# Attention with PV in batches of two key tiles

## Chip, cores, metric

One core of a Trainium2 chip runs the whole program. The time is the device time of one execution in microseconds (us), here the median of several executions.

## What is computed

One transformer layer with conditioning, for 8 sequences of 512 tokens, 512 channels wide, in float32. There are 16 query heads of 32 channels that share 4 key/value heads (four query heads to one key head, called a group below).

```
cond = silu(c) @ wc.T + bc
sh1, sc1, g1, sh2, sc2, g2 = split(cond)
h = ln(x) * (1 + sc1) + sh1
q, k, v = h @ wq.T, h @ wk.T, h @ wv.T
a = softmax(q k / sqrt(32));  attn = a v
x = x + g1 * (attn @ wo.T)
h = ln(x) * (1 + sc2) + sh2
x = x + g2 * (gelu(h @ w1.T + b1) @ w2.T + b2)
```

## The kernel before

A prologue makes the conditioning and turns the weights, then `attention` does all 8 sequences, then `mlp` does all 8. Only `attention` changes.

A sequence is 64 beats: 4 groups (one per key head), in each 4 key tiles `kt` of 128 keys, in each the 4 query heads `r`. Every engine has a `beat` function, and all run the same 64 beats in their own order, tied by semaphores. A beat of TensorE (PE) makes one bank of transposed scores (`scores`, 128 keys by 512 queries), which ScalarE (ACT) turns into `probs[kt]` with an exponential (`exp`), and one matmul of untransposed scores for a later group (`rows`), whose maximum VectorE (DVE) takes (`row_max`). Both sorts of score banks are double-buffered: the scores of beat n need the exponential of beat n-2, the row matmul of beat n the maximum of two rows before. The exponent subtracts the maxima inside the matmul: at beat 10 (`TURN_BEAT`) of a group TensorE turns the maxima of the next group (`turn_max`), ScalarE and VectorE split them into two parts (`max_high`, `max_low`), and at beat 11 ScalarE issues two DMAs (`stack_max`) that put them under `q_stack`, which the first scores of the next group need. A beat with nothing else is two matmuls.

`values` multiplies one key tile's `probs` with `v`: four heads, 32 columns each, into `pv_bank`, two matmuls a head. `sums` does the same with a matrix of ones and `probs_sum`, which GpSimd (POOL) adds up over the key tiles. Before, `values` of tile kt-1 runs in beat 1 of key tile kt (`PV_BEAT`), the last one in beat 1 of the next group, and `sums` behind the `values` of beat 5 (`SUM_AT` is (kt, r) = (1, 1)). `copy_pv` takes the finished bank, then `log_sums`, `invert`, `refine`, `reciprocal`, `divide`, `attn_high` and `attn_low` turn it into `attn`.

The table `FILL` says what else TensorE does in each beat, keyed by (group, key tile), one text per r. T0 to T3 turn the next sequence's x (ScalarE then does `modulate` and `h_high`, VectorE `h_low`), VT turns v, K, Q0 to Q3 and V are projections of the next sequence (Q3 of the present one), O0 to O3 the output projection of the sequence before; the letters a to d are quarters of a projection, three matmuls each. All use two `proj_bank` in the order in which they end, each waiting (`room`) until the one two before was taken. ScalarE takes them one beat after (`ACT_LAG`), VectorE two (`DVE_LAG`); h has lags of two and three. `STATS_AT`, `MOMENTS_AT`, `EPS_AT`, `SHIFT_AT` and `NORM_AT` are the beats (0 to 63) in which the normalization of the sequence after the next is done on VectorE, ScalarE and GpSimd.

The SyncE (SP) queue holds, in order: the copies of k and q into their stacks (`stack_k`, `stack_q`, 12 DMAs each for q), the load of the next x, in group 3 the store of x1 (`store_x1`), and when it has landed the load of the next `resid` (`load_resid`, 1 MB).

Of the kernel before, what the change touches and what calls it, by code (L numbers as in the profile page):

```python
# [16 lines left out]
HKV, R, HD = 4, 4, 32  # L17
DFF = 2048
TT = N // P
# [16 lines left out]


FILL = {
    (0, 0): ("VT", "", "", "Q3abcd"),
    (0, 1): ("T0", "", "", ""),  # L40
    (0, 2): ("T1", "", "T2", ""),
    (0, 3): ("", "", "T3", "O0ab"),
    (1, 0): ("", "O0c", "O0d Ka", ""),
    (1, 1): ("Kb", "", "Kcd", "O1abc"),
    (1, 2): ("O1d", "", "Q0ab", "Q0c"),
    (1, 3): ("", "", "", "Q0d O2a"),
    (2, 0): ("", "", "O2b", "O2c"),
    (2, 1): ("O2d", "", "O3a", "O3b"),
    (2, 2): ("", "O3c", "", "O3d Q1a"),
    (2, 3): ("", "", "Q1bc", "Q1d Q2a"),  # L50
    (3, 0): ("", "", "", "Q2bc"),
    (3, 1): ("", "", "Q2d", ""),
    (3, 2): ("Va", "Vb", "", "Vc"),
    (3, 3): ("", "Vd", "", ""),
}
GROUP = TT * R
PV_BEAT = 1
PV_COPY = 2
SUM_AT = (1, 1)
LN_AT = (2, 0)  # L60
INVERT_AT = (2, 0)
REFINE_AT = (2, 2)
RECIP_AT = (2, 2)
DIVIDE_AT = (2, 3)
# [3 lines left out]
TWO_ROWS = 6  # L68
ACT_LAG, DVE_LAG, COPY_LAG, TURN_LAG = 1, 2, 2, 3
STATS_AT = (40, 41, 43, 44)  # L70
MOMENTS_AT = 47
EPS_AT = 47
SHIFT_AT = 52
NORM_AT = (54, 55, 59, 63)
COND_AT = 2
RESID_AFTER = {0: (0,), 1: (1,), 2: (2, 3)}
# [65 lines left out]
def seq_units(b, has_last, has_next):  # L142
    ahead = before_units().after()
    if has_last:
        ahead = Units(seq_order(False, True), ahead).after()
        step = sizes(seq_order(True, True))
        ahead = {k: (b - 1) * step[k] + ahead[k] for k in ahead}
    return Units(seq_order(has_last, has_next), ahead)


def after_units():
    return Units(["O0", "O1", "O2", "O3"], seq_units(B - 1, True, False).after())
# [315 lines left out]
def attention(nc, f32, f32r, ALU, ACT, AX, sb, ps, sem, as_f32, seq_dram, ident, cond_cols, neg_half, norm_bufs, norm_sems,  # L468
# [3 lines left out]
    with ExitStack() as st:  # L472
# [23 lines left out]
        proj_taken = {"act": sem("proj_taken_act"), "dve": sem("proj_taken_dve")}  # L496
# [16 lines left out]
        def group_no(b, g):  # L513
            return b * HKV + g
# [8 lines left out]
        def exps_no(b, g, kt):  # L523

            return b * (HKV * TT * R) + (g * TT + kt) * R
# [4 lines left out]
        def rowed(b, g, has_next):  # L530

            if g < HKV:
                return b, g
            return (b + 1, g - HKV) if has_next else None
# [16 lines left out]
        with nc.Block() as block:  # L551
# [136 lines left out]
            def _(act):  # L688
# [121 lines left out]
                def beat(b, n, u, has_last, has_next, odd):  # L810

                    g, (kt, r) = n // GROUP, divmod(n % GROUP, R)
                    prev = (b, g - 1) if g > 0 else (b - 1, HKV - 1) if has_last else None
                    first_group = (g == 1 and not has_last)
                    after_turn = rowed(b, g + 1, has_next)
                    exp(b, g, kt, r, has_last)
                    if n % GROUP == TURN_BEAT and after_turn:
                        max_high(*after_turn)
                    if n % GROUP == TURN_BEAT + 1 and after_turn:
                        stack_max(*after_turn)  # L820
                    if prev and (kt, r) == (0, PV_COPY):
                        copy_pv(*prev, is_first=first_group)
                    if prev and (kt, r) == LN_AT:
                        log_sums(*prev, is_first=first_group)
                    if prev and (kt, r) == INVERT_AT:
                        invert(*prev)
                    if prev and (kt, r) == HIGH_AT:
                        if g == 2 and has_last:
                            act.wait_ge(proj_ready, u.ready("O3"))
                        attn_high(*prev, odd)  # L830
                    if n == COND_AT:
                        copy_cond(b + 1)
                    if n == EPS_AT and has_next:
                        add_eps(b + 2)
                    if n == SHIFT_AT and has_next:
                        shift_of(b + 2)
                    if n in NORM_AT and has_next:
                        norm(b + 2, NORM_AT.index(n))
                    for name in ended(n - COPY_LAG, has_last, has_next):
                        if name[0] == "T":  # L840
                            h_high(b + 1, u, int(name[1]))
                    for name in ended(n - ACT_LAG, has_last, has_next):
                        if name == "VT":
                            take_vt(b, u, has_last)
                        elif name == "V":
                            take_v(u)
                        elif name[0] == "T" and has_next:
                            modulate(b + 1, u, int(name[1]))
                        elif name[0] == "T":
                            modulate(b + 1, u, int(name[1]), scale=SC2, shift=SH2)  # L850
                        elif name == "K":
                            k_high(b + 1, u)
                        elif name[0] == "Q":
                            q_high(b if name == "Q3" else b + 1, int(name[1]), u)
# [15 lines left out]
            def _(dve):  # L870
# [101 lines left out]
                def beat(b, n, u, has_last, has_next, odd):  # L972
                    g, (kt, r) = n // GROUP, divmod(n % GROUP, R)
                    prev = (b, g - 1) if g > 0 else (b - 1, HKV - 1) if has_last else None
                    if n == MOMENTS_AT and has_next:
                        dve.wait_ge(stats_done, b * TT + 3 * TT)
                    for row in rows_in(b, n, has_next):
                        if row[2] < ROWS:
                            row_max(*row)
                    if n == MOMENTS_AT and has_next:  # L980
                        moments(b + 2)
# [42 lines left out]
            def _(pe):  # L1024
# [86 lines left out]
                def values(b, g, kt, is_first=False):  # L1111

                    pe.wait_ge(exp_done, exps_no(b, g, kt) + R)
                    if kt == 0 and not is_first:
                        pe.wait_ge(pv_copied, group_no(b, g))
                    for r in range(R):
                        last = nc.tensor.matmul(pv_bank[HD * r:HD * r + HD, :], v[:, kt, g * HD:g * HD + HD],  # L1117
                                                probs[kt][:, r, :], start=(kt == 0), stop=(kt == TT - 1))
                    last.then_inc(pv_done, 1)

                def sums(b, g, is_first=False):

                    pe.wait_ge(added, group_no(b, g) * (TT - 1) + (TT - 1))
                    if not is_first:
                        pe.wait_ge(attn_split, group_no(b, g))
                    for r in range(R):
                        last = nc.tensor.matmul(sum_bank[HD * r:HD * r + HD, :], ones[:, :], probs_sum[:, r, :],
                                                start=True, stop=True)
                    last.then_inc(sums_ready, 1)
# [33 lines left out]
                def beat(b, n, u, has_last, has_next, odd):  # L1163
                    g, (kt, r) = n // GROUP, divmod(n % GROUP, R)
                    prev = (b, g - 1) if g > 0 else (b - 1, HKV - 1) if has_last else None
                    scores(b, g, kt, r, has_last)
                    for row in rows_in(b, n, has_next):
                        if row[2] < ROWS:
                            rows(*row)
                    if r == PV_BEAT and kt > 0:  # L1170
                        if (g, kt) == (0, 1):
                            pe.wait_ge(proj_taken["act"], u.taken("VT"))
                        values(b, g, kt - 1, is_first=not has_last and g == 0)
                    elif r == PV_BEAT and prev:
                        values(*prev, TT - 1)
                    for name, tiles in fill(n, has_last, has_next):
                        do(name, tiles, b, u, odd)
                    if (kt, r) == SUM_AT and prev:
                        sums(*prev, is_first=not has_last and g == 1)
                    for row in rows_in(b, n, has_next):  # L1180
                        if row[2] == ROWS:
                            turn_max(*row[:2])
# [5 lines left out]

                def after(b):
                    u = after_units()  # L1190
                    values(b, HKV - 1, TT - 1)
                    for tt in range(2):
                        out_part(b, tt, u, range(HKV - 1), True)
                    sums(b, HKV - 1)
                    for tt in range(2):
                        out_part(b, tt, u, range(HKV - 1, HKV), True)
                    for tt in range(2, TT):
                        out_part(b, tt, u, range(HKV), True)
# [309 lines left out]
```

## Time and profile before

| | |
|---|---|
| median of 3 runs | 1560.06 us (1552.71 to 1562.45) |
| the profiled execution | 1565.58 us, its span 1563.8 us |
| TensorE, VectorE, ScalarE, GpSimd busy | 95%, 51%, 40%, 37% |
| mean granted TensorE clock | 0.975 of full |

Busy shares are averages over the whole span; matmuls overlap, so their starts tell more than their durations. Times in rows are us from the start of the span.

### The profile page before, as it was taken

Reading aid. Unit: us, or ns where it says so; the run is one execution under the profiler, and the core shown is the slowest. Engines: PE = TensorE matmul, PEld = TensorE weight load, DVE = VectorE, ACT = ScalarE, POOL = GpSimd, SP = SyncE. Lnnn points to the kernel's source line nnn. Section 1 sums busy time; section 2 is a strip of 40 time slices with the busy share of each in tenths; the row PEclk is TensorE's granted clock in tenths of the full one; section 3 lists DMA queues with packets and bytes.
Section 4 is the critical chain, followed back from the end, with each engine's and each line's share of the span. In section 5 each row is a group of like instructions: output and inputs, shape, how many; then the busy total and the mean of one; then the engine's idle time right before and its main releaser. Section 6 shows DMA issues by size and latency. Waiting matters only on the chain. (4 is left out here: it accounts for less than half of the span.)

```text
span 1563.8 us, 19142 instructions
## 1 busy us (share of the span) xinstructions
PE 1481.9 (95%) x7013; PEld 1045.6 (67%) x7013; DVE 800.6 (51%) x1356; ACT 625.1 (40%) x1116; POOL 576.0 (37%) x222
## 2 busy tenths in 40 slices
PE   7889999998999999998979999999999999999996
PEld 4545556555656555654448888888788888878885
DVE  5377667776776677676544342332524242242421
ACT  5346656665575666666532322112111121211210
POOL 0027567675776677576710020110202021020202
PEclk9869999999999999999999999999999999999998
DMA  7132314233151313323053311010202001020100
GB/s 259 55 75 59 97 52 117 65 85 101 33 154 36 112 54 98 93 71 87 2 158 112 101 55 34 27 60 0 87 0 69 18 27 60 0 87 0 61 1 27
DMA packets 68309, 105.16 MB, mean 67 GB/s; under 512 B 10464, under 2 KB 19696, under 8 KB 68232
## 3 DMA queue, kind: packets, MB, share of 16 engines
q1 hardware_dynamic: 66192, 103.74, 21.7%
q8 instruction: 40, 0.66, 0.2%
q10 hardware_dynamic: 2048, 0.53, 0.2%
q14 instruction: 29, 0.24, 0.0%
HBM read 55.44 MB, written 16.81 MB: 46 GB/s over the span
## 5 line engine op out<-in xcount | busy, mean ns | idle before, releaser
L899 DVE TENSOR_REDUCE neg_max<-row_bank 128x1 f32<-128x512 f32 x512 | 338.5, 683 | 184.1 <-PE row_bank L1095 181.9
L768 ACT ACTIVATE probs<-key_bank 128x512 f32<-128x512 f32 x512 | 301.5, 597 | 224.5 <-PE key_bank L1108 219.6
L1463 PE MATMUL acc<-w_t,hidden 128*128 128x512 f32 x1536 | 370.6, 390 | 7.7 <-DVE hidden L1380 7.7
L1453 PE MATMUL up<-h,w_t 128*128 128x512 f32 x1536 | 370.9, 391 | 0.0
L1463 PEld LDWEIGHTS acc<-w_t,hidden 128*128 128x128 f32 x1536 | 287.3, 188 | 69.8 <-DVE hidden L1380 10.7
L1453 PEld LDWEIGHTS up<-h,w_t 128*128 128x128 f32 x1536 | 287.5, 188 | 58.7
L651 POOL TENSOR_TENSOR probs_sum<-probs_sum,probs 128x2048 f32<-128x2048 f32 x62 | 284.5, 4589 | 29.2 <-ACT probs L768 22.5
L1324 ACT ACTIVATE gelu_full<-up,bias_cols 128x512 f32<-128x512 f32 x128 | 88.3, 690 | 515.2 <-PE up L1453 515.2
L1378 DVE CAST hidden<-gelu_full 128x512 fp32r<-128x512 f32 x128 | 67.2, 525 | 443.4 <-ACT gelu_full L1324 441.7
L1108 PE MATMUL key_bank<-q_stack,k_stack 98*128 98x512 f32 x512 | 227.0, 446 | 21.4 <-DMA q_stack<-max_row 13.3
L1095 PE MATMUL row_bank<-k_stack,q_stack 96*128 96x512 f32 x512 | 212.0, 426 | 10.8 <-DVE neg_max L899 9.5
L1281 POOL TENSOR_TENSOR y<-y,gate_now 128x512 f32<-128x512 f32 x32 | 47.4, 1482 | 454.9 <-DVE y L1388 454.9
L651 POOL TENSOR_TENSOR probs_sum<-probs 128x2048 f32<-128x2048 f32 x31 | 142.7, 4602 | 175.9 <-ACT probs L768 175.9
L1108 PEld LDWEIGHTS key_bank<-q_stack,k_stack 98*128 98x128 f32 x512 | 97.9, 192 | 145.2 <-ACT probs L768 57.7
L1117 PE MATMUL pv_bank<-probs,v 128*32 128x512 f32 x1024 | 139.3, 617 | 0.7 <-ACT probs L768 0.7
L1095 PEld LDWEIGHTS row_bank<-k_stack,q_stack 96*128 96x128 f32 x512 | 101.0, 197 | 46.8 <-DVE neg_max L899 26.9
L1040 PE MATMUL proj_bank<-wo_t,attn 128*128 128x512 f32 x384 | 107.6, 404 | 4.9 <-DVE attn L940 4.9
L1380 DVE TENSOR_TENSOR hidden<-gelu_full,hidden 128x512 fp32r<-128x512 f32 x128 | 102.1, 798 | 4.4
L1040 PE MATMUL proj_bank<-h,wq_t 128*128 128x512 f32 x384 | 99.4, 393 | 0.0
L1040 PEld LDWEIGHTS proj_bank<-wo_t,attn 128*128 128x128 f32 x384 | 72.3, 192 | 34.4 <-issue 12.6
L1040 PEld LDWEIGHTS proj_bank<-h,wq_t 128*128 128x128 f32 x384 | 72.4, 189 | 16.2
L1271 POOL TENSOR_TENSOR rstd<-var_eps,neg_half 128x4 f32<-128x4 f32 x7 | 7.1, 1017 | 193.9 <-DVE var_eps L1347 193.9
(117 smaller groups left out, 1069.0 us busy)
## 6 DMA issues: line engine op xcount, KB each, us to landing
q_stack<-spare SPq DMA_DIRECT2D x384, 64.0 KB, 2.0
xa<-in_x_dram SPq DMA_DIRECT2D x8, 1024.0 KB, 5.1
resid<-in_x_dram SPq DMA_DIRECT2D x8, 1024.0 KB, 7.9
x_scratch<-resid SPq DMA_DIRECT2D x8, 1024.0 KB, 4.4
xa<-x_scratch SPq DMA_DIRECT2D x8, 1024.0 KB, 5.7
spare<-in_L_cond_w_dram SPq DMA_DIRECT2D x32, 256.0 KB, 3.0
resid<-x_scratch SPq DMA_DIRECT2D x8, 1024.0 KB, 6.8
out_dram<-y SPq DMA_DIRECT2D x8, 1024.0 KB, 4.2
```

Of the source, the lines that this page charges most:

```text
L651: nc.gpsimd.tensor_tensor(probs_sum[:, :, :], first_in[:, :, :], probs[kt][:, :, :], ALU.add).then_inc(added, 1)
L768: nc.scalar.activation(probs[kt][:, r, :], key_bank[r % 2][:, :], ACT.Exp).then_inc(exp_done, 1)
L899: nc.vector.tensor_reduce(out=neg_max[:, g % 2, i:i + 1], in_=row_bank[(g + i) % 2][:, :], op=ALU.max, axis=AX.X, negate=True).then_inc(ro ...
L1040: last = nc.tensor.matmul(bank, lhs(i, kt), rhs(j, kt), start=(kt == 0 and (i, j) == (0, 0)), stop=(kt == KD - 1 and (i, j) == (1, 0)))
L1095: nc.tensor.matmul(row_bank[(g + i) % 2][:, :], q_stack[0:STACK, g, r, qt * P:qt * P + P], k_stack[0:STACK, g, :], start=True, stop=True). ...
L1108: nc.tensor.matmul(key_bank[r % 2][:, :], k_stack[0:SHIFT, g, kt * P:kt * P + P], q_stack[0:SHIFT, g, r, :], start=True, stop=True).then_i ...
L1117: last = nc.tensor.matmul(pv_bank[HD * r:HD * r + HD, :], v[:, kt, g * HD:g * HD + HD], probs[kt][:, r, :], start=(kt == 0), stop=(kt == T ...
L1324: nc.scalar.activation(gelu_full[j % 2][:, :], up[j % 2][:, :], ACT.Gelu, bias=bias_cols[:, j:j + 1]).then_inc(gelu_done, 1)
L1378: nc.vector.tensor_copy(hidden[j % 2][0][:, :], gelu_full[j % 2][:, :]).then_inc(hid_hi, 1)
L1380: nc.vector.tensor_tensor(hidden[j % 2][1][:, :], gelu_full[j % 2][:, :], as_f32(hidden[j % 2][0][:, :]), ALU.subtract).then_inc(hid_split, 1)
L1453: last = nc.tensor.matmul(up[j % 2][:, :], w1_t[i][:, kt, j * P:j * P + P], h[k][:, kt, :], start=(kt == 0 and n == 0), stop=(kt == KD - 1 ...
L1463: last = nc.tensor.matmul(acc[tt][:, :], hidden[j % 2][i][:, tt * P:tt * P + P], w2_t[k][:, j, :], start=(j == 0 and n == 0), stop=(j == N ...
```

## The change

`values` is no longer called once per key tile. `PV_AT` names two beats of a group: beat 5, where it is called for tiles 2 and 3 of the group before, with `sums` right behind, and beat 11, where it is called for tiles 0 and 1 of the present group. `copy_pv` moves from beat 2 to beat 5, `invert` from beat 8 to beat 9. The table of fill is laid out anew with the same tokens, and the steps of the normalization move: moments and eps from 47 to 51, shift from 52 to 54. Behind the last sequence `values` is called for two tiles.

```diff
@@ -36,29 +36,29 @@
 
 
 FILL = {
-    (0, 0): ("VT", "", "", "Q3abcd"),
-    (0, 1): ("T0", "", "", ""),
-    (0, 2): ("T1", "", "T2", ""),
-    (0, 3): ("", "", "T3", "O0ab"),
-    (1, 0): ("", "O0c", "O0d Ka", ""),
-    (1, 1): ("Kb", "", "Kcd", "O1abc"),
-    (1, 2): ("O1d", "", "Q0ab", "Q0c"),
-    (1, 3): ("", "", "", "Q0d O2a"),
-    (2, 0): ("", "", "O2b", "O2c"),
-    (2, 1): ("O2d", "", "O3a", "O3b"),
-    (2, 2): ("", "O3c", "", "O3d Q1a"),
-    (2, 3): ("", "", "Q1bc", "Q1d Q2a"),
-    (3, 0): ("", "", "", "Q2bc"),
-    (3, 1): ("", "", "Q2d", ""),
-    (3, 2): ("Va", "Vb", "", "Vc"),
+    (0, 0): ("Q3a", "Q3b", "Q3cd", "T0"),
+    (0, 1): ("", "", "VT", ""),
+    (0, 2): ("T1", "T2", "", ""),
+    (0, 3): ("", "T3", "O0a", ""),
+    (1, 0): ("O0b", "O0cd Kab", "Kc", "Kd"),
+    (1, 1): ("", "", "O1a", "O1b"),
+    (1, 2): ("O1c", "O1d Q0ab", "Q0c", ""),
+    (1, 3): ("", "Q0d", "", "O2a"),
+    (2, 0): ("O2b", "O2c", "", "O2d"),
+    (2, 1): ("", "", "O3a", "O3b"),
+    (2, 2): ("O3c", "O3d Q1a", "", ""),
+    (2, 3): ("", "Q1bc", "", "Q1d"),
+    (3, 0): ("Q2a", "", "Q2b", "Q2c"),
+    (3, 1): ("", "", "Q2d", "Va"),
+    (3, 2): ("", "Vb", "Vc", ""),
     (3, 3): ("", "Vd", "", ""),
 }
 GROUP = TT * R
-PV_BEAT = 1
-PV_COPY = 2
+PV_AT = {(1, 1): (-2, -1), (2, 3): (0, 1)}
+PV_COPY = (1, 1)
 SUM_AT = (1, 1)
 LN_AT = (2, 0)
-INVERT_AT = (2, 0)
+INVERT_AT = (2, 1)
 REFINE_AT = (2, 2)
 RECIP_AT = (2, 2)
 DIVIDE_AT = (2, 3)
@@ -68,9 +68,9 @@
 TWO_ROWS = 6
 ACT_LAG, DVE_LAG, COPY_LAG, TURN_LAG = 1, 2, 2, 3
 STATS_AT = (40, 41, 43, 44)
-MOMENTS_AT = 47
-EPS_AT = 47
-SHIFT_AT = 52
+MOMENTS_AT = 51
+EPS_AT = 51
+SHIFT_AT = 54
 NORM_AT = (54, 55, 59, 63)
 COND_AT = 2
 RESID_AFTER = {0: (0,), 1: (1,), 2: (2, 3)}
@@ -818,7 +818,7 @@
                         max_high(*after_turn)
                     if n % GROUP == TURN_BEAT + 1 and after_turn:
                         stack_max(*after_turn)
-                    if prev and (kt, r) == (0, PV_COPY):
+                    if prev and (kt, r) == PV_COPY:
                         copy_pv(*prev, is_first=first_group)
                     if prev and (kt, r) == LN_AT:
                         log_sums(*prev, is_first=first_group)
@@ -1167,16 +1167,17 @@
                     for row in rows_in(b, n, has_next):
                         if row[2] < ROWS:
                             rows(*row)
-                    if r == PV_BEAT and kt > 0:
-                        if (g, kt) == (0, 1):
-                            pe.wait_ge(proj_taken["act"], u.taken("VT"))
-                        values(b, g, kt - 1, is_first=not has_last and g == 0)
-                    elif r == PV_BEAT and prev:
-                        values(*prev, TT - 1)
+                    for tile in PV_AT.get((kt, r), ()):
+                        if tile < 0 and prev:
+                            values(*prev, TT + tile)
+                        elif tile >= 0:
+                            if g == 0 and tile == 0:
+                                pe.wait_ge(proj_taken["act"], u.taken("VT"))
+                            values(b, g, tile, is_first=not has_last and g == 0)
+                    if (kt, r) == SUM_AT and prev:
+                        sums(*prev, is_first=not has_last and g == 1)
                     for name, tiles in fill(n, has_last, has_next):
                         do(name, tiles, b, u, odd)
-                    if (kt, r) == SUM_AT and prev:
-                        sums(*prev, is_first=not has_last and g == 1)
                     for row in rows_in(b, n, has_next):
                         if row[2] == ROWS:
                             turn_max(*row[:2])
@@ -1188,6 +1189,7 @@
 
                 def after(b):
                     u = after_units()
+                    values(b, HKV - 1, TT - 2)
                     values(b, HKV - 1, TT - 1)
                     for tt in range(2):
                         out_part(b, tt, u, range(HKV - 1), True)
```

## Rows read from the trace of the kernel before

**Rows 1.** Page, part 1: busy us (share of the span) and instructions of each engine.

```profile
PE 1481.9 (95%) x7013; PEld 1045.6 (67%) x7013; DVE 800.6 (51%) x1356; ACT 625.1 (40%) x1116; POOL 576.0 (37%) x222
```

**Rows 2.** Stretches: us, busy by engine (instructions), granted clock, DMA share, GB/s.

```profile
266.40:355.40 89.00, 85.16 (x434) 50.81 (x433) 63.91 (x108) 57.06 (x109) 64.35 (x20) 1.00 0.34 99
...
711.90:802.00 90.10, 79.19 (x386) 40.02 (x387) 53.80 (x78) 52.53 (x98) 48.48 (x14) 0.98 0.21 63
```

**Rows 3.** Waits of PE, 98 to 802 us: us in total, times, longest.

```profile
PE key_bank L1108 <- DMA q_stack<-max_row: 13.3, 5, 3.8
PE key_bank L1108 <- ACT probs L768: 5.8, 18, 0.5
PE proj_bank L1040 <- DVE attn L940: 4.9, 1, 4.9
PE row_bank L1095 <- DVE neg_max L899: 3.1, 10, 0.3
```

**Rows 4.** Timeline of PE, 430 to 438 us: start us, us, instruction.

```profile
430.68 0.40 PE L1108 MATMUL key_bank<-q_stack,k_stack 98*128 98x512 f32 x1
430.92 0.40 PE L1095 MATMUL row_bank<-k_stack,q_stack 96*128 96x512 f32 x1
431.25 1.06 PE L1117 MATMUL pv_bank<-probs,v 128*32 128x512 f32 x8
432.13 1.04 PE L1127 MATMUL sum_bank<-probs_sum,ones 128*32 128x512 f32 x8
433.11 0.50 PE L1108 MATMUL key_bank<-q_stack,k_stack 98*128 98x512 f32 x1
433.45 0.63 PE L1095 MATMUL row_bank<-k_stack,q_stack 96*128 96x512 f32 x2
...
436.50 0.40 PE L1095 MATMUL row_bank<-k_stack,q_stack 96*128 96x512 f32 x1
436.83 1.06 PE L1117 MATMUL pv_bank<-probs,v 128*32 128x512 f32 x8
437.83 0.50 PE L1040 MATMUL proj_bank<-h,wv_t 128*128 128x512 f32 x1
```

**Rows 5.** Timeline of PE: turned maxima and first scores of two sequences.

```profile
261.03 0.27 PE L1100 MATMUL row_bank<-ident,neg_max 128*16 128x128 f32 x1
...
266.44 0.47 PE L1108 MATMUL key_bank<-q_stack,k_stack 98*128 98x512 f32 x1
...
346.84 0.27 PE L1100 MATMUL row_bank<-ident,neg_max 128*16 128x128 f32 x1
...
355.38 0.79 PE L1108 MATMUL key_bank<-q_stack,k_stack 98*128 98x512 f32 x1 [2.96 <-DMA q_stack<-max_row]
```

**Rows 6.** Timeline of DVE and ACT, 255 to 268 us, around a turn.

```profile
256.04 2.69 DVE L899 TENSOR_REDUCE neg_max<-row_bank 128x1 f32<-128x512 f32 x4 [1.71 <-PE row_bank L1095]
...
260.00 0.63 ACT L786 ACTIVATE inverse<-inverse 128x512 f32<-128x512 f32 x1
...
262.31 1.15 ACTq L761 DMA_DIRECT2D q_stack<-max_row  x2
263.51 0.81 ACT L708 ACTIVATE xa<-xa,shift_col,rstd 128x512 f32<-128x512 f32 x1 [1.06 <-DVE neg_max L899]
...
265.19 1.11 ACT L768 ACTIVATE probs<-key_bank 128x512 f32<-128x512 f32 x2
```

**Rows 7.** Timeline of SP's queue in the same two sequences: issues.

```profile
263.92 0.44 SPq L560 DMA_DIRECT2D resid<-in_x_dram  x1
...
336.36 7.48 SPq L576 DMA_DIRECT2D q_stack<-spare  x12
343.88 0.58 SPq L564 DMA_DIRECT2D x_scratch<-resid  x1
...
348.69 0.44 SPq L560 DMA_DIRECT2D resid<-in_x_dram  x1
```

**Rows 8.** Stretch behind the wait, columns as in the second group.

```profile
356.00:363.00 7.00, 7.00 (x26) 3.99 (x25) 2.67 (x4) 3.47 (x7) 1.80 (x1) 0.61 0.40 102
```

## The prediction

> **What bounds the kernel now.** I read the busy shares first: TensorE is busy 95% of the span, VectorE 51%, ScalarE 40% [rows 1]. That alone says that only what shortens TensorE's own stream, or what makes TensorE wait, moves the end. Next the stretches by sequence: a sequence of attention takes about 89 us and has TensorE busy for 85.16 us of it; in the last sequence, which has no next one to project for, it is 79.19 of 90.10 us [rows 2]. So for seven sequences out of eight TensorE is the bound, and in the last one ScalarE's exponentials carry part of it. Then the chain of waits of TensorE over the attention part [rows 3]: 13.3 us in 5 waits for the copy of the row maxima into `q_stack` (the first scores of a sequence), 5.8 us in 18 waits for an exponential, 4.9 us once at the very end for `attn`, 3.1 us for VectorE's row maxima. The MLP behind it is untouched by the change and I take it as it is.
>
> **The change part by part.**
>
> *Fewer blocks of narrow matmuls.* Plain score matmuls start 0.24 us apart (430.68 to 430.92). The call `values` starts 0.33 us after the matmul ahead of it (436.50 to 436.83), and what follows it starts 1.00 us later (437.83); where `sums` follows it, that starts only 0.88 us later (431.25 to 432.13), and the first scores behind `sums` start 0.98 us later, with the next matmul 0.34 us behind instead of 0.24 [rows 4]. So a block of such calls costs 0.88 us a call, and its edges cost 0.09 going in, 0.12 going out and 0.10 on the matmul after that: 0.31 to 0.32 us a block. Before, a group of 16 beats has four blocks (PV; PV with `sums`; PV; PV), afterwards two (PV, PV, `sums`; PV, PV). The second PV of a pair isn't in the trace of before; I price it as `sums` behind PV is priced, 0.88 us. The bounds are no saving at all (1.00 + 0.09 + 0.10 again) and 0.32 us a block; I take the latter, since `sums` has the same shapes and follows the same call. Two blocks less in 32 groups is 64; of these I strike four, in the last groups of the last sequence, where TensorE waits for exponentials anyway. 60 x 0.32 = 19.2 us saved.
>
> *The tail.* `after` now runs two `values` behind the last exponential instead of one: + 0.88 us on the path that sets the end, because the 4.9 us wait for `attn` [rows 3] follows from `sums` behind them. + 0.9 us.
>
> *Waits of PV and of its buffers.* Tiles 2 and 3 of the group before run at beat 5, and `probs` 2 is rewritten at beat 8: three beats in between. Tiles 0 and 1 run at beat 11, their exponentials end at beat 7, their buffers are wanted at beat 16. `copy_pv` sits at ScalarE's beat 5 and waits for both PVs; behind it in ScalarE's order is the exponential of beat 6, whose scores TensorE makes only after `sums` (0.98 us), longer than a copy's 0.6 us. All zero, and the cover is `sums`; without it the copy's 0.6 us would show in each group.
>
> *The table.* The same tokens are done, none added. Its effect is on what the double-buffered banks allow: the scores of beat n need the exponential of beat n-2, the row matmul of n needs the row maximum of n-2. VectorE takes about 0.65 us for each of its operations when they stand close (2.69 us for four [rows 6]), ScalarE about 0.5 for an exponential (1.11 us for two [rows 6]), and by my reading 0.55 to 0.65 for `log_sums` or `invert`; an empty beat of TensorE is two starts, 0.47 us. Where beats are empty and the others have two or three operations each, TensorE waits. I walked through beats 5 to 16 of each group with these.
> Group 0: T1 and T2 now stand in consecutive beats, so two `modulate`, two `h_high`, `invert`, the copy and its DMA issues pile up on ScalarE in beats 9 to 11; about 2 us of waiting in beats 9 to 14. Before it is about as much (the waits for exponentials and row maxima of [rows 3], and short ones below the profile's resolution). Zero, give or take 1 us a sequence.
> Group 1: its beats are full; zero.
> Group 2: `gate` of O3 moves from VectorE's beat 13 to 11, onto `divide` and a `tile_stats`, behind `refine` and `reciprocal`; the row matmul of beat 15 then waits 0.35 us. Six sequences: + 2.1 us.
> Group 3: `invert` moves a beat back, to one without any fill before it, and with it come `shift_of` and two `norm` (0.7 us each) in beats 6 and 7. In the trace `invert` ends 0.40 us before the turned maxima (260.00 + 0.63 against 261.03), the two DMA issues follow 1.28 us after them, and ScalarE goes on with `norm` at 263.51 [rows 5, 6]. By my walk `invert` ends 0.57 us after the turn, `refine` and `reciprocal` come before `max_low`, and the DMA issues start 2.25 us after the turn: 0.97 us later than now. ScalarE is blocked as much longer, its exponential of beat 12 ends 4.75 us after the turn, and the scores of beats 14 and 15 wait 0.5 us each. Work between turn and next sequence is 5.1 us as before; so the next sequence starts 6.2 us after the turn where it now starts 5.4 us after it (261.03 to 266.44), or, where it waits for the DMA, later too.
>
> *The race at the end of a sequence.* Where TensorE waits for the DMA, the turn is at 346.84 and the next sequence starts at 355.38, 8.54 us later, against 5.41 us in the sequence before [rows 5]. The queue shows why: the 1 MB load of `resid` is issued at 348.69, 1.85 us after the turn, beside the maxima's copies; in the other sequence it is issued 2.89 us after (263.92), when they were already out at 262.31 and 262.9 [rows 6, 7]. SP gets there by twelve `q_stack` issues (7.5 to 8.5 us), the store of x1 and its landing (4.8 us). In the new table `q_low` of Q1 comes some 0.7 us later behind group 3's start (its beat 0 now holds a quarter of Q2), while the turn is at the same place (13.0 against 13.1 us after that start, when I add up the beats at these prices). So the load moves about 0.8 us away from the turn and the copies move about 1 us away: nearly the same race, slightly worse. I charge 0.95 us for each of seven boundaries, 6.7 us, bounds -13.3 us (all the waits of [rows 3] gone) and +31 us (every one of seven as bad as the worst).
> A rule of the Trainium skill (DMA: Bandwidth & Descriptors, section Queues, rings and completion order) says that each DMA engine goes round between the queue rows that have work, a packet at a time, and that SP and ACT own a row each; by it the small copies on ACT's row would hardly feel the load on SP's, and the late issue would be harmless. The trace speaks against it here: 2.96 us of waiting with the load beside the copies, none with the copies ahead.
>
> *Queues.* The eps step moves from beat 47 to 51, so GpSimd's rstd waits some 1 us, and its `resid` additions end 1 us later; SP's store waits for its own twelve issues until 343.88 anyway [rows 7], 2.5 us after them. Zero; without that cover 1 us at a boundary. The V transposes move from beat 0 to 6 and are taken at 7, long before PV at 11: zero. T1 waits at beat 8 for T0's bank (VectorE beat 6); it takes the place of a row wait there.
>
> **The sum.** -19.2 + 0.9 + 2.1 + 6.7 = -9.5 us. The profiled execution took 1565.6 us, a span of 1563.8 us and 1.8 us around it; the sum puts it at 1556.1 us. It stood 0.35% above the median of the runs, 1560.06 us, so for the median I forecast 1550.5 us.
>
> **The rivals.**
> *The costs of crowding don't come (chance 0.27).* My walk adds up operations at 0.05 us each; if `invert` ends before the turn, group 3 is as before and only the blocks count: -19.2 + 0.9, 1541.8 us. Speaks for it: the other groups already run with DMA issues at 1 to 1.6 us after the turn. The Trainium skill's rule named above would lead here as well, by making late copies harmless.
> *The race is won (0.10).* If the copies leave ahead of the load everywhere, the 13.3 us go, and with them the slower clock behind a long wait: in the 7 us after 356 the granted clock is 0.61 of full, between the levels of 2.4 and 1.2 GHz, after a stretch in which TensorE stood for 2.96 us [rows 5, 8]; some 2.7 us in such a place, and two or three of them. 1541.8 - 13.3 - 8 = 1520 us.
> *The change doesn't do what it says (0.15).* The edges of a block may be filled by something that comes anyway, such as weights that can't be loaded ahead in a second PV; then each call keeps its 1.2 us and the table's costs remain or vanish: about 1560 us.
> *Slower (0.08).* One mechanism: at the end of each sequence the second copy of the maxima leaves after the load of `resid`. It decides from about 2 us between turn and first issue, the point where the load overtakes. The next sequence then starts about 9.7 us after the turn (load issued at 2.65, 7.1 us as now from 348.69 to 355.38 and a little more), a wait of 4.4 us in seven places instead of 13.3 us in five: + 17.5 us, and the slow clock behind each, 3.4 us in place of three times: + 14. With the 18.3 us saved that is + 13 to + 16 us, 1575 us.
>
> **How the numbers follow.** Forecast case 0.40 with 1543 to 1558 us of its own. The range reaches from the second case down by some 10 us and up over the 1560 case: 1532 to 1568 us; it leaves out the race won and the slower case, 0.18. A measurement here can tell about 1% from no change, that is 1544.5 and 1575.7 us. Faster by more: 0.10 of the won race, 0.20 of the second case, 0.05 of the first. Slower by more: 0.07. Within: 0.58.
>
> **What would show it.** Of the blocks: two PVs 0.88 us apart, and the 1024 PV matmuls in 64 blocks of 16; a second PV at 1.0 us or more would refute the saving. Of group 3: the DMA issue of the maxima 2.2 us after the turn, waits of TensorE for an exponential in beats 14 and 15, waits for the maxima's copy of 3 to 4 us at more boundaries than now. If `refine` comes ahead of the turn there, the second case holds. Wrong altogether I would be if TensorE's waits in the attention part come to less than half of the 27 us that [rows 3] add up to, or if a group other than 3 shows a new one of over 0.5 us.

## The result and the profile after

The changed kernel takes 1546.7 us (median of 20 executions, 1541.22 to 1555.24) where the kernel before takes 1561.64 us in the same comparison: ratio 0.9914, 95% interval 0.9893 to 0.9934, that is 14.9 us or 0.86% faster. The forecast was 0.6%. Two executions of the experiments below, 2893.13 us (changed kernel, late load) and 2619.43 us (kernel before), lie far above all others and are in no ratio. The profiled execution has a span of 1547.1 us, 16.7 us less than that of before. Its page, part 1:

```profile
PE 1466.5 (95%) x7013; PEld 1057.3 (68%) x7013; DVE 800.6 (52%) x1356; ACT 622.4 (40%) x1116; POOL 577.0 (37%) x222
```

As many instructions as in [rows 1], and TensorE's busy time is 15.4 us less. The chain of TensorE's waits from 98 to 790 us, in total, times and longest, is the counterpart of [rows 3]:

```profile
PE key_bank L1108 <- DMA q_stack<-max_row: 13.6, 6, 3.9
PE key_bank L1108 <- ACT probs L768: 6.8, 21, 0.7
PE proj_bank L1040 <- DVE attn L940: 4.9, 1, 4.9
PE row_bank L1095 <- DVE neg_max L899: 2.7, 5, 0.8
```

Waiting is what it was. The gain isn't in a wait that went away. The blocks of narrow matmuls, in the timeline of TensorE, show it, to be read beside [rows 4]:

```profile
255.07 0.40 PE L1095 MATMUL row_bank<-k_stack,q_stack 96*128 96x512 f32 x1
255.40 1.92 PE L1117 MATMUL pv_bank<-probs,v 128*32 128x512 f32 x16
257.25 0.50 PE L1108 MATMUL key_bank<-q_stack,k_stack 98*128 98x512 f32 x1
257.59 0.40 PE L1095 MATMUL row_bank<-k_stack,q_stack 96*128 96x512 f32 x1
257.82 0.40 PE L1108 MATMUL key_bank<-q_stack,k_stack 98*128 98x512 f32 x1
...
267.47 0.40 PE L1095 MATMUL row_bank<-k_stack,q_stack 96*128 96x512 f32 x1
267.80 1.92 PE L1117 MATMUL pv_bank<-probs,v 128*32 128x512 f32 x16
269.54 1.04 PE L1127 MATMUL sum_bank<-probs_sum,ones 128*32 128x512 f32 x8
270.51 0.50 PE L1108 MATMUL key_bank<-q_stack,k_stack 98*128 98x512 f32 x1
```

Two PVs take 1.85 us to the next score matmul (255.40 to 257.25), against 1.00 us for one, and 1.74 us where `sums` follows (267.80 to 269.54), 0.87 each. The edges are still 0.09 us before the block (0.33 instead of 0.24), 0.11 in it (1.85 less 1.74) and 0.10 behind it (0.34 instead of 0.24), but they are paid twice in a group instead of four times: the 1024 PV matmuls now stand in 64 blocks of 16 instead of 128 of 8.

The end of group 3 looks otherwise than in [rows 5, 6]. ScalarE and TensorE there, timelines around the turned maxima at 254.72 us:

```profile
254.47 0.65 ACT L786 ACTIVATE inverse<-inverse 128x512 f32<-128x512 f32 x1
...
256.80 1.15 ACTq L761 DMA_DIRECT2D q_stack<-max_row  x2
258.00 0.82 ACT L708 ACTIVATE xa<-xa,shift_col,rstd 128x512 f32<-128x512 f32 x1 [1.80 <-DVE neg_max L899]
258.73 0.58 ACT L768 ACTIVATE probs<-key_bank 128x512 f32<-128x512 f32 x1
```

```profile
254.72 0.27 PE L1100 MATMUL row_bank<-ident,neg_max 128*16 128x128 f32 x1
...
259.35 0.50 PE L1108 MATMUL key_bank<-q_stack,k_stack 98*128 98x512 f32 x1 [0.21 <-ACT probs L768]
...
260.33 0.50 PE L1108 MATMUL key_bank<-q_stack,k_stack 98*128 98x512 f32 x1 [0.23 <-ACT probs L768]
...
261.55 0.50 PE L1108 MATMUL key_bank<-q_stack,k_stack 98*128 98x512 f32 x1 [0.50 <-DMA q_stack<-max_row]
```

`invert` now ends 0.40 us after the turn where it ended 0.40 us before it. The DMA issues follow 2.08 us after the turn (1.28 before), ScalarE goes on only at 258.00, and the scores of beats 14 and 15 wait for its exponentials. The resting times that the profile prints, 0.21 and 0.23 us, are shorter than what the two beats before those scores lose. By the start times it is 0.36 and 0.50 us (beats of 1.53 and 0.97 us where 1.17 and 0.47 are due).

From the starts of the score matmuls I added up the time of each group (six middle sequences; medians of each beat). Fills differ, so each group's quarters of projections stand beside it; a quarter costs 0.70 us (beats of 1.17 against 0.47 us). For before and after the time is that of two runs without the wait at the end of a sequence (below), which otherwise are these two kernels:

```
             group 0 (quarters)  group 1      group 2      group 3     sequence
before       21.86 (6)           23.76 (15)   21.65 (12)   18.57 (7)   85.8 us
after        19.64 (5)           23.89 (16)   20.44 (11)   19.26 (8)   83.2 us
at equal fill     -1.52               -0.57        -0.51        -0.01    -2.6
two edges         -0.64               -0.64        -0.64        -0.64    -2.6
rest              -0.88               +0.07        +0.13        +0.63    -0.05
```

So in the middle sequences the sum is that of the edges, and what is gained besides in group 0 is lost in group 3. The line "two edges" is the priced one, 2 x 0.32 us; the part of each group that is not an edge is the difference.

### The profile page after: what moved, and what is told of

It is laid out like the page before. It is cut to its first block and busy times, and to the rows that moved or that the text cites. A ratio compares the mean times of both kernels' runs of the same rounds, so it can differ in the third digit from the quotient of the medians.

```text
span 1547.1 us, 19142 instructions
## 1 busy us (share of the span) xinstructions
PE 1466.5 (95%) x7013; PEld 1057.3 (68%) x7013; DVE 800.6 (52%) x1356; ACT 622.4 (40%) x1116; POOL 577.0 (37%) x222
## 5 line engine op out<-in xcount | busy, mean ns | idle before, releaser
L1465 PEld LDWEIGHTS acc<-w_t,hidden 128*128 128x128 f32 x1536 | 287.3, 188 | 69.8 <-DVE hidden L1382 10.6
L1108 PE MATMUL key_bank<-q_stack,k_stack 98*128 98x512 f32 x512 | 224.1, 441 | 21.3 <-DMA q_stack<-max_row 13.6
L1117 PE MATMUL pv_bank<-probs,v 128*32 128x512 f32 x1024 | 125.7, 609 | 0.0
L1040 PE MATMUL proj_bank<-h,wq_t 128*128 128x512 f32 x384 | 112.1, 416 | 0.0
L1040 PEld LDWEIGHTS proj_bank<-h,wq_t 128*128 128x128 f32 x384 | 78.0, 203 | 18.2
```

The source lines that it names most:

```text
L1040: last = nc.tensor.matmul(bank, lhs(i, kt), rhs(j, kt), start=(kt == 0 and (i, j) == (0, 0)), stop=(kt == KD - 1 and (i, j) == (1, 0)))
L1108: nc.tensor.matmul(key_bank[r % 2][:, :], k_stack[0:SHIFT, g, kt * P:kt * P + P], q_stack[0:SHIFT, g, r, :], start=True, stop=True).then_i ...
L1465: last = nc.tensor.matmul(acc[tt][:, :], hidden[j % 2][i][:, tt * P:tt * P + P], w2_t[k][:, j, :], start=(j == 0 and n == 0), stop=(j == N ...
```

## The experiments

All ratios are to the kernel before, five rounds each; the changed kernel's is 0.9914. The kernel before took 1560 to 1566 us (medians) beside the different experiments, so where two of them are compared the ratios stand beside the times. First, each part of the change by itself, and the two disputed pieces.

**Pairs with the old table.**

```diff
 PV_AT, PV_COPY as after; FILL, MOMENTS_AT, EPS_AT, SHIFT_AT, INVERT_AT as before, but
-    (0, 0): ("VT", "", "", "Q3abcd"),
-    (0, 1): ("T0", "", "", ""),
+    (0, 0): ("", "", "", "Q3abcd"),
+    (0, 1): ("T0", "", "VT", ""),
```

> PV in pairs as in the changed kernel, but the fill table and the beats of the normalization and of invert as before (only the V transposes go from beat 0 to 6, since v may not be overwritten until the PVs of beat 5). Theory A (each block of narrow matmuls has edges of 0.31 us, 62 to 64 blocks less): the 19 us are saved, less what the beats that lost their PV now wait for VectorE and ScalarE; ratio 0.989 to 0.995. Theory B (the gain comes from the new table's even spread, the edges are hidden): ratio 0.998 to 1.003.

Measured: 1591.41 us, ratio 1.0198 (1.0172 to 1.0224). Slower than before by 2%, which neither theory said. The blocks are halved here too (beat 9 of group 1, without its PV, takes 0.47 us instead of 1.56), but waits took the place of what that saves. Chain of TensorE's waits, 95 to 800 us:

```profile
PE key_bank L1108 <- ACT probs L768: 14.8, 44, 0.7
PE key_bank L1108 <- DMA q_stack<-max_row: 12.6, 7, 4.3
PE row_bank L1100 <- DVE neg_max L899: 7.3, 15, 1.0
PE proj_bank L1050 <- DVE h L883: 6.3, 8, 0.8
```

Two lines are new against [rows 3]: the turn of the maxima waits for the last row maximum, and T1 waits for T0's bank, since VT now stands between them and VectorE comes to T0's `h_low` only behind row maxima (in one such place behind three in a row, with TensorE idle for 0.79 us ahead of T1).

**The table alone.**

```diff
 FILL and all moved steps as after, the calls of values as before, but
-PV_AT = {(1, 1): (-2, -1), (2, 3): (0, 1)}
-PV_COPY = (1, 1)
+PV_BEAT = 1
+PV_COPY = (0, 2)
-    (0, 0): ("Q3a", "Q3b", "Q3cd", "T0"),
-    (0, 1): ("", "", "VT", ""),
+    (0, 0): ("VT Q3a", "Q3b", "Q3cd", "T0"),
+    (0, 1): ("", "", "", ""),
```

> The new table with all its moved steps, but PV as before, one tile in beat 1 of each key tile (V transposes at beat 0, copy of PV at beat 2). Theory A: no edge saved, and the waits of group 0 and 3 change in opposite directions; ratio 0.997 to 1.003. Theory B: the gain is here, ratio 0.990 to 0.994.

Measured: 1583.23 us, ratio 1.0136 (1.0108 to 1.0163). Theory B is out: the table gives nothing by itself, it costs, and more than theory A allowed.

**invert back at beat 8.**

```diff
-INVERT_AT = (2, 1)
+INVERT_AT = (2, 0)
```

> The changed kernel with invert back at beat 8. Theory A (the later invert holds up refine, reciprocal and with them the maxima's DMA issues and ScalarE in group 3): the DMA issue comes back from 2.08 to some 1.5 us after the turn, the waits for exponentials in beats 14 and 15 of group 3 (0.36 and 0.5 us) go; 4 to 6 us less than the changed kernel, ratio 0.988. Rival (the two norms and the shift in beats 6 and 7 crowd it in any case): DMA issue at 2 us still, ratio 0.991.

Measured: 1530.85 us, ratio 0.9814 (0.979 to 0.9839), a gain of 1% where I had expected 0.3 to 0.4%. The scores of beats 14 and 15 no longer wait (beats 13 and 14 take 1.17 and 0.51 us instead of 1.53 and 0.97), but beat 10 takes 1.61 us instead of 1.04, so that group 3 is only 0.27 us shorter, and the DMA issue comes 1.73 us after the turn. The gain is elsewhere: the five stretches at half the clock that the changed kernel has between 170 and 705 us are gone, and the waits for the maxima's copies fell from 13.6 us in 6 to

```profile
PE key_bank L1108 <- DMA q_stack<-max_row: 4.9, 3, 2.4
```

**sums in a block of its own.**

```diff
-                    if (kt, r) == SUM_AT and prev:
+                    if (kt, r) == (1, 2) and prev:
                         sums(*prev, is_first=not has_last and g == 1)
```

> The changed kernel with sums one beat later (beat 6), in a block of its own, so 31 blocks more and nothing else. Theory A: 31 x 0.31 = 9.6 us more than the changed kernel, ratio 0.9975. Theory B: nothing, ratio 0.991.

Measured: 1563.09 us, ratio 1.0009 (0.9993 to 1.0025). In the starts, beats 5 and 6 of group 1 take 2.42 + 2.71 us instead of 3.28 + 1.51: 0.34 us for one block more. That makes 10 us for 31, and 16.4 us were measured (15 by the ratios), more than theory A said; here the waits for the maxima's copies were 16.6 us instead of 13.6.

All four runs differ in those copies' waits as well as in what I had edited. So the race at the end of a sequence had to be taken away.

**resid loaded late, in the changed kernel, with invert at beat 8, and in the kernel before.**

```diff
                     if has_last:
                         store_x1(b - 1)
-                        sp.wait_ge(x1_stored, b * 16)
-                    load_resid(b)
                     if has_next:
                         sp.wait_ge(keys_scored, exps_no(b, 3, 0))
                         stack_k(2)
                         stack_q(u, 2)
+                    if has_last:
+                        sp.wait_ge(x1_stored, b * 16)
+                    load_resid(b)
```

> The changed kernel with SP's queue in another order in group 3: the k and q copies for group 2 first, then the wait for the landed x1 and the load of resid (1 MB). Theory A (the first scores of a sequence wait for the maxima's copies because these share the DMA engines with that load): the 13.6 us of waits for them fall below 3 us, the half clock behind them goes too, some 15 to 20 us less than the changed kernel, ratio 0.979 to 0.982; beats 13 and 14 of group 3 keep their waits for exponentials. Rival (the copies are late because they are issued late, 2.1 to 2.6 us after the turn): the waits stay above 8 us, ratio 0.989 to 0.992.

> The changed kernel with both: the load of resid late and invert at beat 8. Theory A: the 4.9 us of waits that are left with invert at beat 8 go, and the waits in beats 13 and 14 of group 3 are gone, ratio 0.975 to 0.979. Rival: nothing is left to win beside the run with invert at beat 8 alone, ratio 0.981.

> The kernel before with only SP's queue in the other order. Theory A: its 13.3 us of waits fall below 3 us and the half clock behind them goes, ratio 0.985 to 0.989: as much as in the changed kernel, so that the race has no part in what the change gained. Rival: ratio 0.998 or more.

Measured: 1526.0 us, ratio 0.9765 (0.9746 to 0.9785), for the changed kernel; 1526.01 us, 0.9778 (0.9754 to 0.9803), with invert at beat 8; 1543.38 us, 0.9876 (0.9856 to 0.9896), for the kernel before. In none of the three does TensorE wait for the copies once. The call `load_resid` issues two DMAs, `gate_now` (256 KB) and, 0.4 us or more behind it, `resid` (1 MB); "the load" below is the second, and the edit moves both. SP's queue of the changed kernel with the late load, in a sequence whose maxima are turned at 333.71 us:

```profile
331.32 0.58 SPq L564 DMA_DIRECT2D x_scratch<-resid  x1
331.95 2.71 SPq L568 DMA_DIRECT2D k_stack<-spare  x3
334.71 8.62 SPq L576 DMA_DIRECT2D q_stack<-spare  x12
343.38 0.58 SPq L558 DMA_DIRECT2D gate_now<-gate_scratch  x1
344.00 0.46 SPq L560 DMA_DIRECT2D resid<-in_x_dram  x1
```

Here the load is issued 10.3 us after the turn (8.0 to 10.6 at the seven boundaries), and the next sequence starts 6.2 us after the turn at all seven. The maxima's copies are issued as late as ever (2.07 and 2.62 us after the turn), so the rival, late copies, is out. Four to seven `q_stack` copies of 64 KB are under way while the maxima's copies are, and don't hold them up (they land 1.9 to 2.6 us after their issue); it is what `load_resid` issues. Which of its two DMAs does it, the 256 KB or the 1 MB, no run separates. In the two plain kernels the turn and these four events stand so (us after the turn; one column a boundary, the first one left out, where the load comes before the turn):

```
before  load of resid issued   2.89  1.85  2.44  1.83  2.58  1.83   second copy issued 1.86
        next sequence starts   5.41  8.54  6.75  9.36  5.42  8.67
after   load of resid issued   2.95  2.44  3.18  2.63  3.54  2.46   second copy issued 2.62
        next sequence starts   6.83  9.38  7.76 10.23  6.19  9.49
```

With the load 0.7 us or more behind the second copy before, and 0.9 us after, nothing waits; with both at the same time the start comes 3 to 4 us late. The packets in the trace of before say how: at the turn of 346.84 us those of the two copies, 27 ns or less each, come between those of the load and last from 3.45 to 7.86 us after the turn; at the turn of 261.03 us, ahead of the load, from 2.45 to 3.28 us. Between the late and the early load lie 19.4 us in the kernel before and 20.7 us in the changed one (1.2% and 1.5% by the ratios); for the changed kernel that is a little more than I had expected. So the race has no part in the gain: without it the change brings 1543.4 - 1526.0 = 17.4 us.

**Norms earlier.**

```diff
 with the late load:
-SHIFT_AT = 54
-NORM_AT = (54, 55, 59, 63)
+SHIFT_AT = 53
+NORM_AT = (53, 54, 59, 63)
```

> The changed kernel with the late load of resid, and shift and the first two norms one beat earlier (53, and 53 and 54 for 54 and 55), so that one norm falls into the 3.3 us of TensorE's beat 5 of group 3, in which ScalarE stands idle. Theory A (ScalarE's total of work in beats 6 to 12 of group 3 holds up the scores of beats 14 and 15, whichever operation stands where): the 0.36 and 0.50 us of waits there go, 5 to 6 us less than the run with the late load alone, ratio 0.973. Rival (the chain invert, refine, reciprocal, max_low, DMA issue sets ScalarE's time, whatever stands before it): the waits stay, ratio 0.9765.

Measured: 1522.66 us, ratio 0.976 (0.973 to 0.9791), by the median 3.3 us less than with the late load alone, by the ratio not told from it. One of the two waits went (beat 13 takes 1.16 us instead of 1.53), the other stayed (beat 14: 0.96 us). Each theory is half right. (The profiled execution took 1527.78 us; it has a stretch of 6.8 us at half the clock in the first sequence, which the one with the late load alone has not.)

**Pairs with the old table, the table alone, and sums apart, each with the late load.**

> The first experiment (pairs with the old table) again, with the late load of resid, to be read beside the kernel before with that load (ratio 0.9876). Theory A (without the race, the 5 us a sequence of edges saved are eaten by beats that lost their PV and now wait, and by a beat 11 with fill and two PVs): some 20 us more than that kernel, ratio 1.000. Rival (the old table lost only through the race): ratio below 0.99.

> The second experiment (new table, PV singly) with the late load. Theory A: single PVs land in beats that the new table fills (9, 13) and leave beats 11 and 12 empty, some 1.8 us a sequence more than the kernel before with that load, ratio 0.996 to 0.998. Rival: ratio 0.988, the table costs nothing by itself.

> Sums in a block of their own, with the late load, to be read beside the changed kernel with that load (0.9765). Theory A: 31 edges of 0.31 us, 9.6 us more, ratio 0.9825 to 0.984; the rest of the 16 us that sums apart cost with the early load was the race. Rival: the block costs more than its edges, 15 us again, ratio 0.986 or more.

Measured: 1577.3 us, ratio 1.0105 (1.0076 to 1.0134); 1562.51 us, 1.0012 (0.9994 to 1.003); 1536.49 us, 0.9838 (0.9808 to 0.9868). Beside the kernel before with the late load, pairs alone cost 33.9 us and the table alone 19.1 us (2.3% and 1.4% by the ratios), and the two together save 17.4 us. The groups, added up as above:

```
                        group 0 (q.)  group 1 (q.)  group 2 (q.)  group 3 (q.)  sequence
pairs, old table        22.84 (6)     24.16 (15)    22.60 (12)    19.92 (7)     89.5 us
single PVs, new table   21.57 (5)     24.76 (16)    21.85 (11)    19.82 (8)     88.0 us
sums apart              19.92 (5)     24.25 (16)    20.77 (11)    19.72 (8)     84.7 us
```

Both expectations for the mixtures were too mild. For the middle sequences they were near (3.7 us a sequence more, 2.2 us more), but I had counted only six of them: with pairs and the old table the first sequence takes 83.9 us instead of 76.9 and the last 82.3 instead of 77.1, another 12 us. In the old table, beat 11 of groups 1 to 3 holds fill and now two PVs (3.3 to 4.0 us in one beat), while most of beats 1, 9 and 13 are empty; in the new one single PVs come on top of filled beats (O1d Q0ab with PV: 3.73 us) and leave beats 11 and 12 empty, where the scores wait for ScalarE. Waits of the pairs with the old table here:

```profile
PE key_bank L1109 <- ACT probs L769: 19.0, 54, 1.1
PE row_bank L1101 <- DVE neg_max L900: 7.2, 15, 1.1
PE proj_bank L1051 <- DVE h L884: 6.4, 8, 0.8
```

Sums apart came out as expected: 10.5 us for 31 blocks, 0.34 us each (11.4 us by the ratios). So of what it cost with the early load some 3 to 6 us were the race.

**attn_high later.**

```diff
 with the late load and the earlier norms:
-HIGH_AT = (3, 0)
+HIGH_AT = (3, 2)
```

> The run with the earlier norms and the late load, and attn_high moved from beat 12 to beat 14 of a group, behind the exponential of beat 13. Theory (the wait of 0.5 us that is left before the scores of beat 15 in group 3 is attn_high standing ahead of the exponential of beat 13 on ScalarE): that wait goes, and part of the one in group 0 as well; 3 to 5 us less, ratio 0.973. Rival (ScalarE is simply behind by then, after the DMA issues and a norm): the wait stays or moves to the first scores of the next group, ratio 0.976.

Measured: 1523.29 us, ratio 0.9738 (0.9715 to 0.9761), the median as with the earlier norms; the ratio lies nearer to the theory, the intervals of the two runs overlap, and the trace has to decide. Beat 14 fell from 0.96 to 0.56 us, but the last beat of the group rose by 0.13 and the first three of the next sequence from 4.27 to 4.72 us together: the wait moved there. That speaks for the rival.

The late load beats both kernels clearly. Of the versions that have it, those with an earlier norm, with `invert` at beat 8 or with a later `attn_high` can't be told apart from the plain one.

## Why the prediction was right

The time came out within the range and the way that was forecast, and the mechanism that carried the forecast, fewer edges, is the one that the runs show. Several of the smaller terms were wrong, and part of the agreement is luck (see the sum).

*The edges, 60 x 0.32 = 19.2 us.* Right in mechanism and size. Two PVs take 1.85 us, two edges less a group are 0.64 us, groups 1 and 2 became 0.57 and 0.51 us shorter at equal fill, and the reverse edit costs 0.34 us a block (sums apart, with the late load). The rival that the change doesn't do what it says is out. The first sequence I had priced like the others, but without the race it is only 0.4 us shorter (76.9 to 76.5 us) where eight edges less would be 2.6 us. What I didn't see is how far this depends on the table: the same pairs in the old one cost 33.9 us. I had priced the table from the walk alone, and never asked what the pairs would do without it.

*The tail, + 0.9 us.* Wrong in mechanism. At full clock the second PV there costs 0.1 us: from the last scores to `sums` it is 6.68 us with the late load, against 6.58 in the kernel before. Before, TensorE stood 0.69 us for the last exponential ahead of its PV; now the PV of tile 2, which has long been ready, runs in that time. The kernel before and the changed one with the late load:

```profile
790.03 1.07 PE L1117 MATMUL pv_bank<-probs,v 128*32 128x512 f32 x8 [0.69 <-ACT probs L768]
```

```profile
746.86 0.50 PE L1109 MATMUL key_bank<-q_stack,k_stack 98*128 98x512 f32 x1 [0.47 <-ACT probs L769]
747.29 1.92 PE L1118 MATMUL pv_bank<-probs,v 128*32 128x512 f32 x16
749.15 4.46 PE L1041 MATMUL proj_bank<-wo_t,attn 128*128 128x512 f32 x18
```

In the profile of the changed kernel it is 8.32 us:

```profile
770.80 0.51 PE L1108 MATMUL key_bank<-q_stack,k_stack 98*128 98x512 f32 x1 [0.48 <-ACT probs L768]
771.23 3.28 PE L1117 MATMUL pv_bank<-probs,v 128*32 128x512 f32 x16
774.44 4.75 PE L1040 MATMUL proj_bank<-wo_t,attn 128*128 128x512 f32 x18
779.12 1.07 PE L1127 MATMUL sum_bank<-probs_sum,ones 128*32 128x512 f32 x8
```

Here the two PVs take 3.2 us and not 1.85, since TensorE runs at half its clock from 771.7 to 775.1 us. The stretch that holds them shows it, granted clock 0.67 of full:

```profile
770.00:775.00 5.00, 4.52 (x19) 1.22 (x20) 4.01 (x3) 2.27 (x5) 0.00 (x0) 0.67 0.96 299
```

In the kernel before no slow stretch fell on its PV (1.00 us, 790.03 to 791.03), and none on the two in the late-load run, whose TensorE waits for the same exponentials. Of the ten traces with two PVs at the end, six have 6.7 us there and four, with such a stretch, 8.2 to 8.3 us; what makes it fall there stays open. The last sequence itself is 2.3 us shorter (3.0 without the race). That comes from its groups 0 and 1; groups 2 and 3, where I had struck the edges, are 0.3 us shorter and 0.5 us longer.

*Waits of PV, of its buffers and queues, zero.* Right: there is no wait of `pv_bank` or `v` in the chain of waits.

*Group 0, zero give or take 1 us.* This is the term that was most off: 0.88 us a sequence gained, some 6 us in all, at the edge of what I had allowed. The waits lie as in the walk: beats 8, 10, 13 and 14 (1.27, 0.62, 1.06, 1.47 us). But before it had more of them than I took: beats 7, 12, 13 and 14 take 1.05, 1.08, 1.87 and 1.46 us, where 0.47, 0.47, 1.56 (with a PV) and 0.83 are due. With single PVs in the new table beats 12 and 13 take 1.76 and 2.07 us, with the pair in beat 11 they take 0.56 and 1.06. Of the difference in beat 13, 1.09 us is only the PV that stands there; the 1.20 us in beat 12, which is empty in both, is waiting that went. Read with the walk, that the 2.5 us of a pair give ScalarE and VectorE time to finish `invert`, `refine` and the two `modulate` is the likely reason; only the difference is shown.

*Group 2, + 0.35 us a sequence.* Beat 15 took 1.30 us where 1.17 are its due: the wait that I named, at 0.13 us. Group 1, priced at zero, is off by 0.07 us.

*Group 3, + 0.95 us a boundary, and the race.* Nearly right where the waits are (0.36 and 0.50 us at the named scores, forecast 0.5 each; DMA issue 2.08 us after the turn, forecast 2.25; start of the next sequence 6.2 us after the turn without the race, as forecast). In the net it is 0.63 us. The cause that I gave, `invert` one beat later, does not hold: with invert at beat 8 and the late load the time is the same within the runs' spread, and the wait stands before the scores of beat 11 instead. That it is ScalarE's sum of work between beats 6 and 14 is what the three moves suggest (`invert`, `attn_high`, the norms): the first two came back as a wait at another place, and of the third one wait went. No run shows it alone. The race moved as told, both ways (the load 0.6 us later behind the turn on average, the copies 0.76 us), and remained nearly what it was, 13.6 for 13.3 us, at 6 boundaries for 5. The waits of 3 to 4 us at more boundaries that I had named as a sign didn't come: there are three, as before. With the clock the race is worth 20.7 us now and 19.4 us before, within what the runs can tell; I had priced the case of a won race at 21.3 us.
The rule of the Trainium skill that I set against this (DMA: Bandwidth & Descriptors, section Queues, rings and completion order: an engine goes round between the rows that have work) would, as I read it, have made the order of load and copies indifferent. The runs with the late load say that it isn't, by 19 us; the measurement decides. How long an engine stays with one row before it goes on, no run here shows, so what fails may be only my reading of the rule.

*The sum.* -9.5 us forecast, -14.9 us measured. Without the race it is -17.4 us. In the two profiles without it the six middle sequences are together 16.1 us shorter, the last 3.0 and the first 0.4; what is left lies ahead of the first and behind the last. Over them group 0 gave some 6 us that I had at zero, group 3 took some 4 where I charged 6.7, the first sequence gave 2.2 us less than its edges, and the tail took 0.1 us for 0.9. That these errors partly cancel is luck. So is it that the race stayed as it was: I had it change by tenths of a microsecond, and with `invert` one beat earlier, which gains nothing where the race is taken away, changes of that size brought some 16 us.

## What to carry to other kernels

When a bounding engine changes between sorts of matmul, price the edges of a block from start times, since busy shares hide them; they were 0.3 us here against 0.9 us of work. Batching such blocks and spreading the other work over the beats that get empty are one edit: either half alone made this kernel slower. Before comparing versions of a schedule, take out any race that flips by tenths of a microsecond; here large transfers issued beside two small ones were worth more than the whole change, and moving them behind brought no new wait.

## What was not expected of the hardware

Two copies of 8 KB, issued by ScalarE 0.55 us apart, were held up by a load of 1 MB from SP (and the 256 KB ahead of it) by an amount that depends on tenths of a microsecond. In the six traces with the early load (42 boundaries) the second copy landed 1.9 to 2.5 us after its issue where the load came 0.67 us or more behind it (7 boundaries), 3.5 to 5.3 us where it came 0.13 to 0.64 us behind (13), 6.6 to 8.8 us where it came with it or up to 0.54 us ahead (16), and 5.2 to 6.2 us where it came 4 to 5 us ahead (6). The q copies of 64 KB from SP in the same stretch did it no harm (1.9 to 2.8 us in the eight traces with the late load).

In the kernel before, waits of 2.25 to 3.79 us of TensorE at a boundary are followed by 3.4 to 6.8 us at half the clock, and one of 1.20 us isn't. It is no rule: in the changed kernel waits of 1.42 and 1.63 us are followed by 6.8 us of it, and with `invert` at beat 8 one of 2.44 us is not. Of the eight runs with the late load four have no slow stretch between 115 us and the last sequence (the kernel before, the changed one, with `invert` at beat 8, sums apart), the other four have one each.
